# Second stage of a two-layer cross-attention kernel: scores made twice, queries stacked by DMA, in place of transposed probabilities

## What is computed

```python
q = _lora_linear(hidden_states, Wq, Aq, Bq).reshape(bsz, q_len, NH, HD)
k = _lora_linear(traces, Wk, Ak, Bk).reshape(bsz, t_len, NKV, HD)
v = _lora_linear(traces, Wv, Av, Bv).reshape(bsz, t_len, NKV, HD)
...
scores = jnp.einsum('bhqd,bhtd->bhqt', q, k) / jnp.sqrt(jnp.asarray(HD, q.dtype))
attn = jax.nn.softmax(scores, axis=-1)
context = jnp.einsum('bhqt,bhtd->bhqd', attn, v)
...
out = _lora_linear(context, Wo, Ao, Bo)
return hidden_states + out
```

## Time and profile before

| | |
|---|---|
| median of three runs | 1505.43 us |
| the profiled execution, its own time | 1502.18 us |
| its span | 1500.4 us |
| TensorE clock granted, mean | 0.997 |
| busy: TensorE, VectorE, ScalarE, GpSimd | 98%, 60%, 62%, 34% |
| DMA: bytes, packets | 151.63 MB, 85003 |

### The profile page before, as it was taken

How to read it: one execution, slowest core, us unless ns; L and a number is a source line. 1 busy time by engine, 2 the same in 40 slices (tenths; PEclk the granted TensorE clock), 3 DMA queues, 4 the chain that set the end, 5 groups by cost and what they waited for, 6 DMA issues and landing times.

```text
span 1500.4 us, 26103 instructions
## 1 busy us (share of the span) xinstructions
PE 1465.0 (98%) x8295; PEld 1190.8 (79%) x8295; DVE 898.0 (60%) x2137; ACT 937.0 (62%) x3121; POOL 502.8 (34%) x641
## 2 busy tenths in 40 slices
PE   7999999999979999999999999999999999999998
PEld 5788788788767878887888878888888788888876
DVE  5666666666556655565565655655665655656664
ACT  4655656656466666666666666666666666666664
POOL 6433333333343223332233223322332233322330
PEclk9999999999999999999999999999999999999999
DMA  7355556666571211112111211111112111111111
GB/s 195 134 196 177 176 183 215 226 227 223 178 267 51 66 62 55 54 54 67 55 54 68 74 55 54 54 64 59 54 63 73 59 55 54 54 67 55 54 54 59
DMA packets 85003, 151.63 MB, mean 101 GB/s; under 512 B 14530, under 2 KB 49956, under 8 KB 84868
## 3 DMA queue, kind: packets, MB, share of 16 engines
q1 hardware_dynamic: 84868, 149.96, 29.9%
HBM read 99.59 MB, written 50.33 MB: 100 GB/s over the span
## 4 chain that ended last, share of the span: by engine, by line
PE 93%; ACT 3%; DVE 2%; issue 2%; POOL 0%; DMA 0%; SPq 0%; ACTq 0%; DVEq 0%; POOLq 0%
PE bank L462 24%; PE bank L476 23%; PE bank L362 11%; PE bank L489 8%; PE bank L499 7%; PE bank L509 4%; PE bank L422 2%; PE bank L445 2%; PE bank L437 2%; PE bank L312 2%; PE bank L349 2%; PE bank L392 1%; PE bank L399 1%; ACT lora_aT_kv L650 1%; PE bank L404 1%
## 5 line engine op out<-in xcount | busy, mean ns | idle before, releaser
L1105 POOL TENSOR_SCALAR k_diag<-k_in 32x256 fp32r<-32x256 f32 x256 | 227.2, 887 | 683.5 <-PE bank L489 666.5
L719 ACT ACTIVATE prob<-bank,soft 128x128 f32<-128x128 f32 x1024 | 363.5, 371 | 25.3 <-DVE soft L934 20.8
L462 PE MATMUL bank<-wq_hi,hT 128*128 128x512 f32 x1024 | 355.2, 408 | 0.0
L476 PE MATMUL bank<-wo_hi,cT 128*128 128x512 f32 x1024 | 350.9, 403 | 1.5 <-DVE cT L947 1.5
L931 DVE TENSOR_REDUCE soft<-bank 128x4 f32<-128x512 f32 x256 | 176.2, 688 | 283.7 <-PE bank L489 283.6
L728 ACT COPY probT<-bank 128x512 f32<-128x512 f32 x256 | 150.3, 587 | 305.5 <-PE bank L499 305.4
L462 PEld LDWEIGHTS bank<-wq_hi,hT 128*128 128x128 f32 x1024 | 193.0, 188 | 65.6 <-issue 25.2
L476 PEld LDWEIGHTS bank<-wo_hi,cT 128*128 128x128 f32 x1024 | 192.4, 188 | 41.7 <-DVE cT L947 2.4
L719 ACT ACTIVATION_READ_ACCUMULATOR prob<-bank,soft 128x1 f32 x1024 | 212.6, 208 | 0.0
L362 PE MATMUL bank<-wkv_hi,yT 128*128 128x512 f32 x512 | 205.2, 422 | 0.0
L462 PE MATMUL bank<-wq_lo,hT 128*128 128x512 f32 x512 | 202.6, 396 | 0.0
(11 more groups left out here) (145 smaller groups left out, 1968.7 us busy)
## 6 DMA issues: line engine op xcount, KB each, us to landing
h_in<-h_dram SPq DMA_DIRECT2D x64, 512.0 KB, 3.4
y_in<-in_ctx SPq DMA_DIRECT2D x32, 512.0 KB, 3.8
x_in<-in_x SPq DMA_DIRECT2D x32, 512.0 KB, 4.7
h_dram<-h_out SPq DMA_DIRECT2D x32, 512.0 KB, 2.7
out_dram<-h_in SPq DMA_DIRECT2D x32, 512.0 KB, 2.6
k_in<-kT_dram SPq DMA_DIRECT2D x128, 64.0 KB, 2.8
w_raw<-in_L_xattn_Wo SPq DMA_DIRECT2D x65, 64.0 KB, 2.2
w_raw<-in_L_xattn_Wq SPq DMA_DIRECT2D x16, 256.0 KB, 2.7
```

Of the source, the lines that this page charges most:

```text
L462: m = pe.matmul(bank(half), hT[:, part, c, :], w[:, c, half * BANK:(half + 1) * BANK], start=c == 0 and part == 0 and w is wq_hi, stop=c = ...
L476: m = pe.matmul(bank(half), cT[:, part, c, :], w[:, c, half * BANK:(half + 1) * BANK], start=c == 0 and part == 0 and w is wo_hi, stop=c = ...
L719: act.activation(prob[t % 2][:, g, :], score_bank(t)[:, g * P:(g + 1) * P], ACT.Exp, bias=st_t[:, 1, g:g + 1], scale=SCORE1, accum_out=st_ ...
L1105: pool.tensor_scalar(k_diag[rows, q, :, 0, g, :], k_in[rows, q, :, :], 1.0, None, ALU.mult).then_inc(S["kd"], 1)
```

## The change

Scores are made twice. The first time (`scores`, now L528) a head is one product: three bands of 32 rows, queries hi, lo, hi against keys hi, hi, lo, 96 rows deep and 128 columns wide. It serves the maximum and the sum alone; `exponents` writes back into the bank. The second time (`scores_again`, L540) the same two stacks change sides, so that keys lie in rows, four heads of one key head stream as 512 columns, and two more rows subtract the maximum (-1 in the keys' stack, the maximum's hi and lo part in the queries'). ScalarE's exponential of that bank (`probabilities`, L760) is the transposed probability itself, not normalised. The reciprocal of the sums is multiplied in after the context product (`split_context`, L1004).

For this, queries are brought into the stack by 12 DMAs of 32 rows by 2 KB per half (`stack_q`, L1280), keys by 3 (`load_k`, L1292). Maxima and reciprocals, one column a head, are turned once per half (`turn_stats` L479, `stat_rows` L989), written to DRAM, and read back as rows, the reciprocals spread over 32 partitions (`spread_stats`, L1311). The maximum's half k is turned in slot 4k + 4, its first second scores stand in slot 4k + 5, its context product in slot 4k + 9. VectorE takes over copying q out of PSUM (`evacuate_q`, L951). In the first stage VectorE also splits the keys into hi and lo (`rest_kT`). `k_diag`, `turn_prob`, `normalise`, `evacuate_probT` and `keys_diagonal` go. h is reloaded into a buffer of its own (`h_res`). In steady state q is turned in slots 1 and 6, h in slots 3 and 7.

```diff
+        QUERY_ROWS = ((slice(0, HD), 0), (slice(HD, 2 * HD), 1), (slice(2 * HD, 3 * HD), 0))
+        KEY_ROWS = ((slice(0, HD), 0), (slice(HD, 2 * HD), 0), (slice(2 * HD, 3 * HD), 1))
+        MAX_ROWS = slice(3 * HD, 3 * HD + 2)
+        SCORE_ROWS, STACK_ROWS = slice(0, 3 * HD), slice(0, 3 * HD + 2)
         at[0] = shared
         q_sb = sb("q_sb", [P, HID])
-        qT = sb("qT", [P, UNITS, 2, P], F32R)
-        k_diag = sb("k_diag", [P, NQ, 2, 2, 2, P], F32R)
-        k_in = sb("k_in", [P, NQ, 2, P])
+        q_part = sb("q_part", [P, 2, GROUP, P], F32R)
...
+        MAXIMA, AGAIN, CONTEXT = 4, 5, 9
...
+        def turns(b, s):
+            of = {1: (("q", b, 1),), 3: (("h", b + 2, 0),), 6: (("q", b + 1, 0),), 7: (("h", b + 2, 1),)}
+            return [u for u in of.get(s, ()) if u[1] < B]
...
+            if s == 0:
+                return [("o", b - 2, c) for c in (6, 7) if b >= 2]
+            if s < 5:
+                return [("q", b + 1, c) for c in (2 * s - 2, 2 * s - 1)]
+            return [("o", b - 1, c) for c in (2 * s - 10, 2 * s - 9)]
...
+            def turn_stats(k):
+                freed, count = turn_freed["stat", k, 0]
+                pe.wait_ge(freed, count)
+                pe.wait_ge(S["stats_zero"], 1)
+                if k < HALVES:
+                    pe.wait_ge(S["max"], GROUP * (k + 1))
+                pe.wait_ge(S["rec"], k)
+                pe.transpose(TURN[:, 0:P], stats[:, k % 2, :], ident[:]).then_inc(S["turn_mm"], 1)
...
-                b, u = divmod(t, UNITS)
-                if u % GROUP == 0:
-                    pe.wait_ge(S["qT_lo"], 4 * b + 2 * (u // GROUP) + 2)
-                    pe.wait_ge(S["kd"], 8 * (NQ * b + u // GROUP + 1))
+                k, member = divmod(t, GROUP)
+                if member == 0:
+                    pe.wait_ge(S[f"q_in{k % RING}"], 12 * DMA * (k // RING + 1))
+                    pe.wait_ge(S[f"k_in{k % RING}"], 3 * DMA * (k // RING + 1))
                 if t >= 2:
                     pe.wait_ge(S["exp"], GQ * (t - 1))
-                for pair in range(2):
-                    for kpart in range(2):
-                        m = pe.matmul(score_bank(t)[:, pair * 2 * P:(pair + 1) * 2 * P], qT[:, u, pair, :],
-                                      k_diag[:, u // GROUP, pair, kpart, :, :].rearrange("p g t -> p (g t)"),
-                                      start=kpart == 0, stop=kpart == 1)
+                for g in range(GQ):
+                    m = pe.matmul(score_bank(t)[:, g * P:(g + 1) * P], q_stack[SCORE_ROWS, k % RING, g, member, :],
+                                  k_stack[SCORE_ROWS, k % RING, g, :], start=True, stop=True)
                 m.then_inc(S["sc_mm"], 1)
+            def scores_again(n):
+                k, g = divmod(n, GQ)
+                if g == 0:
+                    pe.wait_ge(S["stack_ones"], 1)
+                    pe.wait_ge(S[f"max_in{k % RING}"], DMA * (k // RING + 1))
+                if n >= 2:
+                    pe.wait_ge(S["st_exp"], n - 1)
+                pe.matmul(again_bank(n), k_stack[STACK_ROWS, k % RING, g, :],
+                          q_stack[STACK_ROWS, k % RING, g, :, :].rearrange("p j n -> p (j n)"),
+                          start=True, stop=True).then_inc(S["st_mm"], 1)
+            def context(k):
+                b, q = divmod(k, NQ)
+                pe.wait_ge(S[f"v_in{q}"], DMA * (b + 1))
+                if k:
+                    pe.wait_ge(S["c"], k)
+                pe.wait_ge(S["st_exp"], GQ * (k + 1))
...
+            for t, b, s in slots():
                 if unit_of(t):
                     scores(t)
-                if unit_of(t - 2):
-                    turn_prob(t - 2)
-                if done is not None:
-                    context(done)
...
+                if t % GROUP == 0 and t >= MAXIMA:
+                    turn_stats((t - MAXIMA) // GROUP)
...
+                for kind, of, c in projections(b, s):
+                    if kind == "q":
+                        project_q(of, c)
+                    else:
+                        project_o(of, c)
+                k = half_at(t, CONTEXT)
+                if k is not None:
+                    context(k)
+                if unit_of(t - AGAIN):
+                    scores_again(t - AGAIN)
...
+            def round_q(b, half):
+                k = NQ * b + half
+                if k:
+                    act.wait_ge(S[f"q_in{(k - 1) % RING}"], 12 * DMA * ((k - 1) // RING + 1))
+                act.wait_ge(S["qT_mm"], k + 1)
+                act.copy(q_part[:, 0, :, :].rearrange("p j n -> p (j n)"), TURN).then_inc(S["q_hi"], 1)
...
+            def probabilities(n):
+                k, g = divmod(n, GQ)
+                if k:
+                    act.wait_ge(S["pv_mm"], k)
+                act.wait_ge(S["st_mm"], n + 1)
+                act.activation(probT[:, g, :, :].rearrange("p j n -> p (j n)"), again_bank(n), ACT.Exp,
+                               scale=SCORE1).then_inc(S["st_exp"], 1)
...
+                dve.tensor_scalar(negs[:, t % 2, :], largest, -SCORE1, None, ALU.mult).then_inc(S["neg"], 1)
+            def reciprocals(k):
+                if k:
+                    dve.wait_ge(S["turn_mm"], k)
+                dve.wait_ge(S["exp"], GQ * GROUP * (k + 1))
+                dve.reciprocal(stats[:, (k + 1) % 2, REC],
+                               sums[:, k % 2, :, :].rearrange("p g j -> p (g j)")).then_inc(S["rec"], 1)
+            def stat_rows(k):
+                dve.wait_ge(S["turn_mm"], k + 1)
+                if k < HALVES:
+                    if k:
+                        dve.wait_ge(S["max_out"], DMA * k)
+                    dve.tensor_scalar(max_rows[:, 0, :], TURN[0:HEADS, 0:P], 1.0, None, ALU.mult).then_inc(S["max_hi"], 1)
+                    dve.wait_ge(S["max_hi"], k + 1)
+                    dve.tensor_tensor(max_rows[:, 1, :], TURN[0:HEADS, 0:P], f32(max_rows[:, 0, :]),
+                                      ALU.subtract).then_inc(S["max_lo"], 1)
+                if k:
+                    if k >= 2:
+                        dve.wait_ge(S["rec_out"], DMA * (k - 1))
+                    dve.tensor_scalar(rec_out[REC, :], TURN[REC, 0:P], 1.0, None, ALU.mult).then_inc(S["rec_row"], 1)
+            def split_context(k):
+                b, q = divmod(k, NQ)
+                c_quad = c_sb[:].rearrange("p j n -> p (j n)")
+                if k:
+                    dve.wait_ge(S["c_lo"], k)
+                dve.wait_ge(S["rec_in"], GQ * DMA * (k + 1))
+                dve.wait_ge(S["pv_mm"], k + 1)
+                dve.tensor_tensor(c_quad, bank(6), rec_rows[:].rearrange("p j n -> p (j n)"), ALU.mult).then_inc(S["c"], 1)
...
+            def stack_q(b, half):
                 if b >= B:
                     return
+                k = NQ * b + half
+                sp.wait_ge(S["q_lo"], k + 1)
+                if k >= RING:
+                    sp.wait_ge(S["st_mm"], GQ * (k - RING + 1))
+                for g in range(GQ):
+                    for rows, part in QUERY_ROWS:
+                        sp.dma_start(f32(q_stack[rows, k % RING, g, :, :]),
+                                     f32(q_part[g * HD:(g + 1) * HD, part, :, :])).then_inc(S[f"q_in{k % RING}"], DMA)
+            def load_k(k):
+                if k >= HALVES:
+                    return
+                b, q = divmod(k, NQ)
                 sp.wait_ge(S[f"kv_out{b % 2}"], 2 * DMA * (b // 2 + 1))
...
+                if k >= RING:
+                    sp.wait_ge(S["st_mm"], GQ * (k - RING + 1))
+                for rows, part in KEY_ROWS:
+                    sp.dma_start(f32(k_stack[rows, k % RING, :, :]), kT_dram[b, part, :, q * P:(q + 1) * P].rearrange(
+                        "(g d) t -> d g t", g=GQ)).then_inc(S[f"k_in{k % RING}"], DMA)
...
+            def spread_stats(k):
+                if k < HALVES:
+                    sp.wait_ge(S["max_lo"], k + 1)
+                    sp.dma_start(max_dram[k].rearrange("a h n -> h a n"), f32(max_rows[:])).then_inc(S["max_out"], DMA)
+                if k:
+                    sp.wait_ge(S["rec_row"], k)
+                    sp.dma_start(rec_dram[k - 1], rec_out[REC, :]).then_inc(S["rec_out"], DMA)
+                if k < HALVES:
+                    sp.wait_ge(S["max_out"], DMA * (k + 1))
+                    sp.dma_start(f32(q_stack[MAX_ROWS, k % RING, :, :, :].rearrange("p g j n -> p (g j n)")),
+                                 max_dram[k].rearrange("a h n -> a (h n)")).then_inc(S[f"max_in{k % RING}"], DMA)
+                if k:
+                    sp.wait_ge(S["rec_out"], DMA * k)
+                    if k >= 2:
+                        sp.wait_ge(S["c"], k - 1)
+                    for g in range(GQ):
+                        rows = rec_dram[k - 1, g * GROUP:(g + 1) * GROUP, :].rearrange("(a j) n -> a (j n)", a=1)
+                        sp.dma_start(rec_rows[g * HD:(g + 1) * HD, :, :].rearrange("p j n -> p (j n)"),
```

(22 more changed lines are left out.)

374 lines of the change are left out of this document (159 added, 215 removed), and 2 rows, old and new, of the table S.

## The result

The changed kernel takes **1675.05 us** (median of 4 runs, 1670.53 to 1676.69) against 1505.54 us before: 1.1123 times as long, 95% interval 1.1100 to 1.1147, slower by 170 us. The forecast was 1577 us with a range of 1500 to 1640: the direction was right, the size outside the range. The profiled execution took 1670.53 us, its span is 1668.7 us.

The account below looks back on a forecast made before the run. The prediction took TensorE, busy 98% of the span, to bound the kernel; 1502 - 32 (PE) + 62 (queue wait) + 27 (clock) + 15 (head and tail) = 1574, given as 1577 us for the median, range 1500 to 1640.

Parts of the forecast that it names:

- PE's own work: TensorE, second stage: cheaper products less two statistics transposes save 1.0 us a batch, 32 us in all.
- Rival (a): TensorE's scores: 128-column products don't fall below a 512-column one; about 1640 us, chance 0.25.
- SP's queue: SyncE's DMA queue: twelve query copies at 0.47 us each make PE wait 2.0 us a batch, 62 us in all.
- the product's price: TensorE: a 128-column float32r product, bounded by 0.11 us from below and 0.23 from above, taken at 0.11.
- Second half: Second query stack of a batch: lands at 16.1 us against slots lasting 16.3; costed at nothing, at most 1 us a batch.
- The clock: TensorE behind waits: a fall of the granted clock costs 1.7 us; half of 53 us taken, 27.
- Head and tail: Start and end of the second stage: query stacks, a DRAM round trip and three slots cost 5 to 25 us, 15 taken.
- rival (c): Second scores: the maxima's round trip through DRAM ends last; 1640 us, or 1600 partly replacing the query wait; chance 0.08.
- (b): SyncE's queue: issues at 0.29 us or less keep up, no wait is left; 1478 us, chance 0.14.

Follow-up runs that it names:

- pool6: Changed kernel with rounded-part copies started earlier; SyncE issues those of three head groups, GpSimd the fourth's and the rest of all four; 1484.62 us.
- skip9: Changed kernel with only nine of the twelve query copies issued per half once the ring of three is filled; 1570.7 us.
- skip8: Changed kernel with only eight of the twelve query copies issued per half once the ring of three is filled; 1539.7 us.
- hifirst: Changed kernel with the eight copies of the rounded part issued after ScalarE's rounding only, the four of the rest behind them, all on SyncE; 1657.67 us.
- skip10: Changed kernel with only ten of the twelve query copies issued per half once the ring of three is filled; 1617.8 us.
- via3: Changed kernel with the turned queries written to DRAM by one DMA and read back by three, in place of twelve copies; 1666.87 us.

## Why the prediction was right or wrong

**PE's own work (-1.0 us a batch): right in sign, low.** A batch less its waits and the clock's excess takes 32.2 us, or 32.0 in pool6, against 33.59: -1.4 to -1.6. The four products of 128 columns take 0.10 each (a group starts 0.39 to 0.40 us before what follows it), the 512-column one 0.23, as taken; the transpose of the statistics costs 0.08 (slot 4, which has one, takes 3.56 us, slot 2 without it 3.48), where I took 0.15. Rival (a), that the small float32r products are no cheaper than a large one, fell.

**SP's queue, the step that failed: "0.47 each for the rest, gap included".** It was taken from the loads of w_raw, of the same shape but out of DRAM. The copies inside SBUF cost 0.59, 0.63 with the gap. The other pieces of the chain were right: queries ready after 2.45 us (2.6 forecast), landing 2.0 (2.2), PE there after 7.8 (7.9). Eleven gaps of 0.16 us more make 1.8 us, and the stall was 3.73 in place of 2.0: 50 us over the 29 batches of the table. The text had the bounds of the product's price, with both ends kept for the range, but took the price of the issue from one kind of row without an upper bound, though a dearer row, 0.60 for the loads of k_in, stands in the earlier trace rows and was used for the keys alone; that is why the range ended at 1640. skip9, with a stall of 1.86 us, near the 2.0 forecast, took 1570.7 us, against 1574 in the prediction's sum. That agreement is luck in part: the clock there cost 10 us, not 27, and PE saved 45, not 32, while head and tail cost some 47, not 15.

**Second half, "costed at nothing": 0.12 us a batch, by luck.** The twelve were put to start 8.7 us after slot 0 and to land at 16.1, with slots 0 to 3 lasting 16.3. In the median they started at 7.8, and by the same missed price (7.5 us for the run) landed near 16.7. Slots 0 to 3 last 16.1 us where the clock holds (skip8), which would not have covered it. It was covered because slot 0 ran at the lower clock in every batch; in the batches of hifirst in which the clock held, the wait was 1.1 us.

**The clock, "between none (0) and all (53 us) I take half, 27".** The size of one fall was right (1.7 taken, 1.6 measured). The share was not independent of the wait: behind 3.7 us it fell in every batch, 1.66 x 29 = 48 us, where the forecast had 25 for as many. At the stall that I had forecast, about a fifth of the batches would have lost anything (skip9: 6 of 28).

**Head and tail, "between 5 and 25 us, I take 15": 53.** The head cost 25.4 us. The first scores came 7.4 us later, behind the first stack of twelve copies. In batch 0 PE waited 4.9 us for the second stack, 10.15 for the maxima behind wo_lo's 4 MB and 7.4 for the stack of batch 1; it was busy 20.9 of its 43.7 us, where the kernel before was busy 21.0 of 25.7. The wait for the maxima I had not seen, although it is rival (c) in one place. The tail cost 27.3. The last two batches by windows (columns as above), before, after and in pool6:

```profile
1425.02:1457.72 32.70, 32.70 (x185) 26.53 (x184) 19.03 (x41) 21.06 (x82) 10.73 (x16) 1.00 0.14 45
1457.72:1500.40 42.68, 35.09 (x197) 26.89 (x195) 20.61 (x45) 20.31 (x81) 2.62 (x4) 1.00 0.17 64
```

```profile
1566.00:1602.83 36.83, 32.99 (x162) 25.37 (x162) 16.22 (x36) 17.80 (x74) 0.00 (x0) 0.93 0.37 103
1602.83:1668.70 65.87, 47.85 (x193) 34.46 (x193) 21.67 (x48) 19.84 (x78) 0.00 (x0) 0.83 0.25 75
```

```profile
1391.40:1422.63 31.23, 31.23 (x163) 24.18 (x162) 16.22 (x36) 17.83 (x74) 6.21 (x12) 1.00 0.44 122
1422.63:1482.30 59.67, 44.32 (x194) 32.13 (x193) 21.62 (x48) 20.36 (x79) 2.94 (x6) 0.89 0.27 83
```

PE's idle time there (window less busy time) is 7.6 us before, 21.9 in the change and 15.4 in pool6; its busy time grows from 67.8 to 80.8 and 75.6 us, for fewer instructions (382, then 355 and 357), while the granted clock of the last stretch is 0.83 and 0.89, against 1.00. So of the 27 us some 12 went with the queue, and 15 stay. That these are the longer way from scores to context (maxima through DRAM, a second product, reciprocals through DRAM), with too little other work beside it, fits pool6's idle time there, of which waits for VectorE's cT ended 9.1 us and waits for ScalarE's probT 2.1, but no run took that way apart, so it stays argued.

**The sum again.** Over the 29 batches of the table: -1.4 for PE, +3.84 for the two stalls, +1.66 for the clock, +4.1 a batch, 118 us; the forecast had -1.0 + 2.0 + 0.87 = 1.9, or 54. Of the 64 between them 50 are the price of the issue, 23 the clock behind the longer stall, 3 the second half, and PE gives 12 back. (The table has 115.5, since batch 1 of the kernel before was slow itself.) The rest of the program cost 53 us where the forecast's sum of 72 leaves 18 for it. So 96 us were missed, 50 of them through the one price and 23 more through the clock behind the longer stall.

**Rivals.** (b), that the queue keeps up at 0.29 us an issue or less, fell: 0.507 was the cheapest. Its outcome, though, is what pool6 makes true by a second queue: 1478 was put for a kernel without the wait, 1482 to 1485 was measured. (c) held in the head alone: everywhere else the maxima were in time. Of the signs named for the forecast, PE's idle time before the first scores of each batch, ended by L1289, the lower clock in the second stage and the transposes without idle time were seen; L1289's 0.43, the wait of 2 us and a period of 34.5 to 36 were not.

## What to carry to other kernels

Count the issues of a queue between the moment the data is ready and the moment it is needed, and price them from rows with the same source, not only the same shape: a copy inside SBUF cost 0.63 us of SyncE's time here where a load from DRAM cost 0.45. If the run of issues is longer than the lead, split it over an idle engine's queue before anything else: six copies on GpSimd, with the rounded part started before the rest was ready, turned +11% into -1.3%, where fewer, larger transfers through DRAM gained almost nothing. A wait on TensorE is to be priced together with its clock, and the two are not independent: behind about 1 us nothing was lost, behind 3.7 us 1.6 us more in nearly every batch. And where two runs of issues follow each other, a slow stretch behind the first can hide that the second is late too. What reads as "no wait" may be a wait covered by another loss.

## What the runs showed of the hardware

- An issue of a 32 x 2 KB copy took 0.59 us on SyncE from SBUF and 0.42 from DRAM, to the same destination; 0.61 on ScalarE's queue and 0.50 on GpSimd's, both from SBUF. I had not expected the source to matter, nor GpSimd to be the cheapest.
- With both queues at work the landing of such a copy rose from 2.0 to 2.5 to 2.7 us (up to 6.6), and the pitch of the issues did not change.
- A write of 16 KB took 9.3 us to land beside 4 MB of loads, against 1.7; a write of 512 KB to DRAM 3.0, up to 5.1.
- In the runs with mean stalls of 2.4 to 3.1 us (skip10, via3, hifirst) slot 0 lost nothing, 1.6, or 2.5 to 3.1 us, each of them in the same kernel; in the change (3.7 us) it lost 1.6 in 26 of 28 batches and 2.4 and 2.8 in the other two.
